# Split products in the wide attention layer: fp32 score and value products replaced by three fp32r products each, the next value projection and the context loads moved

## The reference

```python
q = jnp.einsum('bsd,ed->bse', x, wq)
k_new = jnp.einsum('bsd,ed->bse', x, wk)
v_new = jnp.einsum('bsd,ed->bse', x, wv)
k = jnp.concatenate([k_cache, k_new], axis=1)      # k_cache = v_cache = context
v = jnp.concatenate([v_cache, v_new], axis=1)
scores = jnp.einsum('bqd,bkd->bqk', q, k) * scale
attn = jax.nn.softmax(scores, axis=-1)
out = jnp.einsum('bqk,bkd->bqd', attn, v)
return jnp.einsum('bqd,ed->bqe', out, wo)
```

## Time and profile before

| | |
|---|---|
| median of 3 runs | 3709.82 us (3708.83 to 3711.08) |
| span of the profiled execution (its own time) | 3708.5 us |
| TensorE busy | 3396.1 us (92%) |
| VectorE busy | 2402.3 us (65%) |
| ScalarE busy | 1673.8 us (45%) |
| mean granted clock of TensorE | 0.963 |
| this layer | about 2993 to 3345 us |

### The profile page before, as it was taken

The page is one execution under the profiler, slowest core; times in us unless marked ns, Lnnn a source line. Parts: engine busy times, 40 slices in busy tenths (PEclk is TensorE's granted clock), DMA queues, the critical chain, the costliest instruction groups (busy, mean ns, idle before and its releaser), DMA issues. The chain is left out here.

```text
span 3708.5 us, 54381 instructions
## 1 busy us (share of the span) xinstructions
PE 3396.1 (92%) x17963; PEld 2692.7 (73%) x17976; DVE 2402.3 (65%) x6378; ACT 1673.8 (45%) x4027; POOL 955.0 (26%) x997
## 2 busy tenths in 40 slices
PE   6884999998799999999999988999999889988999
PEld 4552787786678787778787766888878656656887
DVE  4888889887576666766666657899755522228433
ACT  4553545444334434444434333788557633331222
POOL 3654444443222222332222223000323400000000
PEclk9886999999999999999999998999999899999999
DMA  5113001001100000110000006999800133333000
GB/s 219 21 19 78 0 0 46 23 0 56 51 20 20 27 20 27 65 42 21 27 20 27 19 17 218 356 406 401 290 27 2 46 118 105 117 97 102 11 10 20
DMA packets 113696, 296.11 MB, mean 80 GB/s; under 512 B 38033, under 2 KB 42129, under 8 KB 107777
## 3 DMA queue, kind: packets, MB, share of 16 engines
q1 hardware_dynamic: 107376, 276.39, 21.2%
q0 software_dynamic: 6160, 17.67, 1.6%
HBM read 251.65 MB, written 41.68 MB: 79 GB/s over the span
## 5 line engine op out<-in xcount | busy, mean ns | idle before, releaser
L40 PE MATMUL bank<-w,cross_ctx_part 128*125 128x512 f32 x1536 | 517.1, 418 | 8.1 <-DVE cross_qn L1090 4.7
L40 PEld LDWEIGHTS bank<-w,cross_ctx_part 128*125 128x125 f32 x1536 | 281.7, 187 | 93.7 <-DVE cross_kn L1090 14.7
L1000 ACT ACTIVATE cross_prob<-bank,cross_neg_max 112x375 f32<-112x375 f32 x256 | 147.2, 575 | 359.3 <-DVE cross_neg_max L1096 359.3
L40 PE MATMUL bank<-w_low,cross_ctx_part 128*125 128x512 f32 x768 | 303.7, 395 | 0.0
L40 PE MATMUL bank<-moe_wt,moe_zT 128*128 128x448 f32 x1176 | 264.0, 373 | 2.1 <-DVE moe_zT L1726 1.5
L1096 DVE TENSOR_REDUCE cross_neg_max<-bank 112x1 f32<-112x375 f32 x256 | 134.0, 524 | 198.0 <-PE bank L872 195.4
L1716 DVE TENSOR_TENSOR moe_wt<-moe_raw,moe_wt 128x1792 fp32r<-128x1792 f32 (+1 forms) x111 | 231.8, 2107 | 16.9 <-ACT moe_wt L1614 16.3
L40 PE MATMUL bank<-w,self_xq 128*112 128x512 f32 x512 | 213.7, 417 | 25.0 <-DVE w_low L595 25.0
L40 PEld LDWEIGHTS bank<-moe_wt,moe_zT 128*128 128x128 f32 x1176 | 215.1, 190 | 17.6 <-issue 1.7
L40 PE MATMUL bank<-mlp_zT,mlp_signs 128*128 128x448 f32 x1024 | 220.8, 368 | 4.7 <-DVE mlp_zT L2329 4.7
L772 POOL TENSOR_TENSOR cross_ve<-cross_mv,eps 125x4 f32<-125x4 f32 (+1 forms) x160 | 32.2, 201 | 730.4 <-DVE cross_mv L1081 730.4
(11 more groups left out here) (398 smaller groups left out, 8403.9 us busy)
## 6 DMA issues: line engine op xcount, KB each, us to landing
moe_raw<-in_moe_w SPq DMA_DIRECT2D x74, 896.0 KB, 7.3
moe_raw<-in_moe_w SPq DMA_DIRECT2D x37, 1024.0 KB, 8.2
stream<-in_L1f SPq DMA_DIRECT2D x32, 768.0 KB, 4.3
cross_ctx_raw<-in_ctxT SPq DMA_DIRECT2D x32, 750.0 KB, 4.1
wide_ctxT<-in_ctxT SPq DMA_DIRECT2D x16, 750.0 KB, 12.8
wide_ctx_rows<-in_ctx SPq DMA_DIRECT2D x16, 750.0 KB
expert_rows<-a_zeros SPq DMA_DIRECT2D x1, 8960.0 KB, 27.0
moe_zrow<-expert_rows SPq DMA_DIRECT2D x35, 256.0 KB, 7.7
```

The lines of the kernel that those rows point to most:

```text
L40: mm = pe.matmul(out, a, b, start=first and n == 0, stop=last and n == len(pairs) - 1)
L1000: op = act.activation(prob[:, t % SLOTS, i, :], score_bank(t)[0:S, i * NK:(i + 1) * NK], ACT.Exp, bias=neg_max[:, h:h + 1], accum_out=tota ...
```

## The change

Scores and value product become split products. For that, `ctxT`, the context rows, the turned q and k, v and the probabilities each get a high part (ScalarE) and a low part (VectorE). The turned keys go into one tile `allT` with the context's, padded by a zero column to 488, so that the scores are one set of 12 products. TensorE makes the v rows of b + 1 ahead of the value product of b. SyncE issues `load` (ctxT and the rows, now waiting for the low parts of the element before) ahead of `load_mlp`. The copy of the context for b + 1 stands on ScalarE between the exponential of b and the copies of q and k of b + 1; `rows_high(b + 1)` stands between `take_v(b + 1)` and the sums of b.

```diff
@@ SyncE
             def load(b):
-                wait(sp, s["scores_in_psum"], b)
+                wait(sp, s["ctxT_low"], b)
                 sp.dma_start(ctxT[:], ...).then_inc(s["ctxT_landed"], 16)
+                wait(sp, s["rows_low"], b)
+                sp.dma_start(ctx_rows[:], ...).then_inc(s["ctx_landed"], 16)
+
+            def load_mlp(b):
                 wait(sp, s["mlp_summed"], 3 * b)
                 sp.dma_start(stream[:, 0:MLP_COLS], io["L1f"][b]).then_inc(s["mlp_landed"], 16)
-                wait(sp, s["out_in_psum"], b)
-                sp.dma_start(ctx_rows[:], ...).then_inc(s["ctx_landed"], 16)
+            load(0)
             sp.wait_ge(s["w_low"], 4)
-            load(0)
+            load_mlp(0)
...
             for b in range(1, B):
                 load(b)
+                load_mlp(b)
@@ TensorE
+            def scores(b):
+                pe.wait_ge(s["ctxT_low"], b + 1)
+                pe.wait_ge(s["q_low"], b + 1)
+                pe.wait_ge(s["k_low"], b + 1)
...
+                wait(pe, s["exp_done"], b)
+                for c in range(DC):
+                    mm = product(pe, ps[3][0:S, 0:NK + 1], [h[:, c, :] for h in qT], [h[:, c, :] for h in allT],
+                                 c == 0, c == DC - 1)
+                mm.then_inc(s["scores_in_psum"], 1)
+
+            def weigh_rows(b):
+                pe.wait_ge(s["rows_low"], b + 1)
+                pe.wait_ge(s["v_low"], b + 1)
+                pe.wait_ge(s["probsT_low"], b + 1)
+                wait(pe, s["out_ready"], b)
+                for j in range(J + 1):
+                    n = JN if j < J else S
+                    mm = product(pe, ps[5][0:S, :], [h[0:n, j, :] for h in probT],
+                                 [h[:, j, :] for h in rows_part] if j < J else [h[:] for h in v], j == 0, j == J)
+                mm.then_inc(s["out_in_psum"], 1)
...
-                    wait(pe, s["probsT_ready"], 2 * b)
+                    wait(pe, s["probsT_low"], b)
...
                 pe.wait_ge(s["exp_done"], b + 1)
                 if one_more:
-                    pe.wait_ge(s["q_ready"], b + 2)
+                    pe.wait_ge(s["q_low"], b + 2)
...
-                for j in range(J + 1):
-                    n = JN if j < J else S
-                    mm = pe.matmul(ps[5][0:S, :], probT[0:n, j, :], ctx_rows[:, j, :] if j < J else v[:],
-                                   start=j == 0, stop=j == J)
-                mm.then_inc(s["out_in_psum"], 1)
                 if one_more:
+                    pe.wait_ge(s["v_low"], b + 1)
                     rows(b + 1, 2, wv, "v_in_psum")
+                weigh_rows(b)
@@ ScalarE
             def take_v(b):
                 act.wait_ge(s["v_in_psum"], b + 1)
-                act.activation(v[:], ps[2][0:S, :], ACT.Copy).then_inc(s["v_ready"], 1)
+                wait(act, s["out_in_psum"], b)
+                act.activation(v[0][:], ps[2][0:S, :], ACT.Copy).then_inc(s["v_ready"], 1)
+
+            def ctxT_high(b):
+                act.wait_ge(s["ctxT_landed"], 16 * b + 16)
+                wait(act, s["scores_in_psum"], b)
+                act.activation(allT[0][:, :, 0:KEYS], ctxT[:], ACT.Copy).then_inc(s["ctxT_high"], 1)
+
+            def rows_high(b):
+                act.wait_ge(s["ctx_landed"], 16 * b + 16)
+                wait(act, s["out_in_psum"], b)
+                act.activation(rows_part[0][:], ctx_rows[:], ACT.Copy).then_inc(s["rows_high"], 1)
...
                 if one_more:
+                    ctxT_high(b + 1)
                     take_rows(b + 1)
                     take_turned(b + 1)
...
+                if two_more:
+                    act.wait_ge(s["v_in_psum"], b + 2)
+                    z_high(b + 2)
                 if one_more:
                     take_v(b + 1)
-                if two_more:
-                    z_high(b + 2)
+                    rows_high(b + 1)
                 sum_magnitudes(b)
@@ VectorE, in step
                 dve.reciprocal(inverse[:], total[:]).then_inc(s["inverse_ready"], 1)
+                if one_more:
+                    ctxT_low(b + 1)
+                    turned_low(b + 1)
                 if not first:
                     add_out(b - 1)
+                probsT_low(b)
+                if not first:
                     measure_next(b - 1)
+                if two_more:
+                    z_low(b + 2)
...
                 dve.tensor_scalar(o[:], ps[5][0:S, :], inverse[:], None, ALU.mult).then_inc(s["out_ready"], 1)
-                if two_more:
-                    z_low(b + 2)
+                if one_more:
+                    v_low(b + 1)
+                    rows_low(b + 1)
```

More of the change, by code:

```diff
@@ L1908, in wide_attention_layer @@
              "out_ready", "outT_in_psum", "out_high", "out_low", "y_in_psum", "x_done", "mlp_landed", "mlp_summed",
-             "next_stat", "next_centre", "next_vareps", "next_rooted", "ahead_landed")
+             "next_stat", "next_centre", "next_vareps", "next_rooted", "ahead_landed", "ctxT_high", "ctxT_low", "q_low",
+             "k_low", "rows_high", "rows_low", "v_low", "probsT_low", "padded")
     s = {n: k.sem(f"wide_{n}") for n in names}
@@ L1919, in wide_attention_layer @@
         ctx_rows = sb("ctx_rows", [JN, J, D])
+        allT = [sb(f"allT{i}", [P, DC, NK + 1], F32R) for i in range(2)]
+        rows_part = [sb(f"rows_part{i}", [JN, J, D], F32R) for i in range(2)]
         q = sb("q", [S, D])
         key = sb("key", [S, D])
-        qT = sb("qT", [P, DC, S])
-        kT = sb("kT", [P, DC, S])
-        v = sb("v", [S, D])
+        qT = [sb(f"qT{i}", [P, DC, S], F32R) for i in range(2)]
+        v = [sb(f"v{i}", [S, D], F32R) for i in range(2)]
         prob = sb("prob", [S, NK])
-        probT = sb("probT", [JN, J + 1, S])
+        probT = [sb(f"probT{i}", [JN, J + 1, S], F32R) for i in range(2)]
         neg_max = sb("neg_max", [S, 1])
@@ L1947, in load @@
             def load(b):
-                wait(sp, s["scores_in_psum"], b)
+                wait(sp, s["ctxT_low"], b)
                 sp.dma_start(ctxT[:], io["ctxT"][b].rearrange("p (c n) -> p c n", c=DC)).then_inc(s["ctxT_landed"], 16)
+                wait(sp, s["rows_low"], b)
+                sp.dma_start(ctx_rows[:], io["ctx"][b].rearrange("(j p) d -> p j d", p=JN)).then_inc(s["ctx_landed"], 16)
+            def load_mlp(b):
                 wait(sp, s["mlp_summed"], 3 * b)
                 sp.dma_start(stream[:, 0:MLP_COLS], io["L1f"][b]).then_inc(s["mlp_landed"], 16)
-                wait(sp, s["out_in_psum"], b)
-                sp.dma_start(ctx_rows[:], io["ctx"][b].rearrange("(j p) d -> p j d", p=JN)).then_inc(s["ctx_landed"], 16)
+            load(0)
             sp.wait_ge(s["w_low"], 4)
-            load(0)
+            load_mlp(0)
             for m in range(MLP_SLOTS):
@@ L1964, in _ @@
         def _(pool):
+            for part in allT:
+                pool.memset(part[:, :, NK:NK + 1].bitcast(F32), 0.0).then_inc(s["padded"], 1)
             for b in range(B):
@@ L2007, in project_out @@
                 mm.then_inc(s["y_in_psum"], 1)
+            def scores(b):
+                pe.wait_ge(s["ctxT_low"], b + 1)
+                pe.wait_ge(s["q_low"], b + 1)
+                pe.wait_ge(s["k_low"], b + 1)
+                if b == 0:
+                    pe.wait_ge(s["padded"], 2)
+                wait(pe, s["exp_done"], b)
[13 more added lines that the diff above has]
+                mm.then_inc(s["out_in_psum"], 1)
             def step(b, one_more, two_more):
                 first = isinstance(b, int) and b == 0
[L2011 to L2019, removed]
+                scores(b)
                 if one_more:
@@ L2085, in take_turned @@
                 act.wait_ge(s["qT_in_psum"], b + 1)
-                act.activation(qT[:], tiled(4), ACT.Copy).then_inc(s["q_ready"], 1)
+                wait(act, s["scores_in_psum"], b)
+                act.activation(qT[0][:], tiled(4), ACT.Copy).then_inc(s["q_ready"], 1)
                 act.wait_ge(s["kT_in_psum"], b + 1)
-                act.activation(kT[:], tiled(0), ACT.Copy).then_inc(s["k_ready"], 1)
+                act.activation(allT[0][:, :, KEYS:NK], tiled(0), ACT.Copy).then_inc(s["k_ready"], 1)
             def take_v(b):
                 act.wait_ge(s["v_in_psum"], b + 1)
-                act.activation(v[:], ps[2][0:S, :], ACT.Copy).then_inc(s["v_ready"], 1)
+                wait(act, s["out_in_psum"], b)
+                act.activation(v[0][:], ps[2][0:S, :], ACT.Copy).then_inc(s["v_ready"], 1)
+            def ctxT_high(b):
+                act.wait_ge(s["ctxT_landed"], 16 * b + 16)
+                wait(act, s["scores_in_psum"], b)
+                act.activation(allT[0][:, :, 0:KEYS], ctxT[:], ACT.Copy).then_inc(s["ctxT_high"], 1)
[3 more added lines that the diff above has]
+                act.activation(rows_part[0][:], ctx_rows[:], ACT.Copy).then_inc(s["rows_high"], 1)
             def out_high(b):
@@ L2115, in step @@
```

(39 more changed lines are left out.)

## The result

The changed kernel takes 3748.7 us (median of 4 runs, 3748.1 to 3756.8) against 3710.5 us of the kernel before (4 runs): ratio 1.0098, 95% interval 1.0086 to 1.0111, which is 32 to 41 us slower. The forecast was 3746 us with a range of 3713 to 3768. The execution that was profiled is the slowest of the four (3756.8 us), and 12.4 us of its 46.6 us more than the profiled one of before stand ahead of this layer (first scores at 3005.78 in place of 2993.38 us), where the change does nothing; the layer is therefore compared by its own length.

A forecast was written before the change was run, and what follows sets the result against it. TensorE's own order bounded the kernel before; after the change, a loop through ctxT's late landing would. 19.2 + 14 x 24.9 + 20.4 = 388.2 us against 351.7, +36.5, gives 3746 us (8 in 10: 3713 to 3768).

The forecast's parts named there:

- The work without waits: TensorE's own work in one element with no new waits: 19.2 us, 2.4 us less than before.
- the 0.85 us ahead of the value product: TensorE's wait for the context rows' DMA; claimed to go because the rows load one element ahead.
- The landing of ctxT: Next element's ctxT lands 10.66 us after the scores' start, 6.3 us after the MLP tile's issue.
- The closed loop: Elements 1 to 14: the transfer burst waits for the value product's end, which depends on the burst; element 22.9 us.
- The pause: TensorE idle 4.0 us ahead of the turn of q in each element, ready at 8.7, started at 12.7.
- The clock: Low TensorE clock behind each pause: 2.0 us an element (1.4 to 2.6), making the element 24.9 us.
- The ends: Element 0 at 19.2 us in place of 21.85, element 15 at 20.4 us in place of 27.1.
- The clock did not hold: Rival: TensorE's clock stays up behind the pauses, element 22.9 us, kernel 3718 us; chance 0.12.
- The two transfers did not run abreast: Rival: ctxT lands 4.5 us after its own issue, pause 2.6 us, element 21.5, kernel 3699 us; chance 0.08.
- the share of 0.89: DMA engines' busy share ascribed to the MLP tile alone, held against the abreast rival: little left for a second transfer.
- The wait was not hidden: Rival: the wait for ctxT is hidden after all, element 19.2 us, kernel 3667 us; chance 0.06.
- ctxT did not land as late as before: Rival: ctxT lands 12.8 us after its issue as before, 6.9 us more an element, kernel 3843 us; chance 0.06.

The follow-up runs named there:

- e1: Changed kernel with SyncE issuing the context tiles of element b + 1 ahead of the MLP tile of b: 3680.4 us, ratio 0.9917 to the kernel before.
- e2: Changed kernel with copy and subtraction of the next ctxT moved behind the copies of q, k and turned q, k: 3667.1 us, 0.9893 to the kernel before.
- e7: Changed kernel with both the late copy of ctxT and the context tiles issued ahead of the MLP tile: 3686.3 us, 0.9892 to the kernel before.
- e8: Changed kernel with the late copy of ctxT, run again on a second chip: 3684.0 us, ratio 0.9895 to the kernel before.
- e6: Late-copy kernel with scores and value product as plain fp32 products over the high parts alone: 3703.3 us, ratio 0.9936 to the kernel before.
- e5: Kernel before with only the context rows' load issued ahead of the MLP tile, products left plain: 3715.4 us, ratio 0.9977 to the kernel before.
- e4: Changed kernel with SyncE loading only the first half of each MLP tile: 3724.7 us, ratio 1.0043 to the kernel before.
- e3: Changed kernel with 16 extra useless products ahead of the turn of q in elements 1 to 14: 3726.2 us, ratio 1.0041 to the kernel before.

## Why the prediction was right

**The work without waits.** Scores 2.7 us forecast, 2.65 measured (3101.42 to 3104.07); value product 2.85 forecast, 2.79 measured; v rows 2.85 and 2.86; element without new waits 19.2 forecast, 19.03 measured in e1, e2, e7 and e8. For the split products the sum had 0.6 us at the scores and 0.6 at the value product and the v rows behind it, 1.2 together; e6 shows 1.27.

**One cover was misread.** The prediction let the 0.85 us ahead of the value product go because the rows load sooner. e5 shows that the load takes away only what lies above 0.51 us; the 0.51 are ScalarE's copy of the probabilities, and what hides that is the v rows, which now stand between. The sum came out right because the change does both.

**The landing of ctxT.** Forecast 10.66 us after the scores' start, with 6.3 us between the MLP issue and the landing. Measured: ScalarE starts its copy at 10.75, and the issue is at 4.38 (forecast 4.36). The closed loop is shown by e1 and e2, which open it at two different places, and by e4, which shortens it in one place and gets the amount back.

**The pause.** 4.0 us forecast, 4.00 mean measured; e3 gives an element of 22.73 us for the pause without the clock, forecast 22.9. That is 3.70 above the 19.03: behind the pause the turn of k no longer waits for ScalarE as it does without it (0.48 us from the turn of q to the turn of k in e3, 0.85 in the earlier trace rows), which gives 0.37 of the 4.0 back. The prediction had this term.

**The clock.** 2.0 us forecast, 1.70 measured by e3 and by the busy time; over 14 elements that term was 4 us too large.

**The ends.** Here the sizes were off. Element 0 was put at 19.2 us and took 22.76: it has no output projection and no transposed output, so that without waits it is 17.03 us (e2), and its own wait for ctxT behind the five MLP tiles, with the low clock behind it, costs 5.7 us; the prediction had named that wait and given it no price beyond "18 to 22 is possible". Element 15 took 21.14 in place of 20.4:

```profile
3376.18 4.57 PE L40 MATMUL bank<-wide_wo,wide_oT 128*112 128x512 f32 x12 [2.39 <-DVE wide_oT L2189]
...
3382.78 2.31 PE L40 MATMUL bank<-wide_rows_part,wide_probT 125*112 125x512 f32 x9 [1.62 <-DVE wide_probT L2215]
```

The wait for the rows' DMA ahead of the value product is gone, as forecast, but 1.62 us stay there for the new low part of the probabilities, and the output projection waits 2.39 us, where it waited 1.39 before. The clock falls here too (mean 0.92). The prediction had the 1.62 us and the 1.0 added to the other at nothing.

**The sum.** 22.76 + 342.06 + 21.14 = 386.0 us against 388.2 forecast: +3.6 from element 0, -6.5 from the elements (the clock, and an element without waits of 19.03 in place of 19.2), +0.7 from the last. The misses cancel in part. The timed medians differ by 38.3 us, 4.0 more than the layer; that rest lies outside the layer and is in no term of the sum. So the mechanism and its sizes were right to some 2 us of the layer, and that the kernel's time came out within 3 us of the forecast is in part luck.

**The rivals.** The clock did not hold: it fell behind 14 of 14 pauses. The two transfers did not run abreast: 6.3 us from the MLP issue to ctxT's landing, where abreast would have been 4.9. The argument held against this rival was weaker than it looked: the share of 0.89 in the earlier trace rows is not of the MLP tile alone, since SyncE issued it at 3321.36 and the rows at 3321.73, both before that stretch. The wait was not hidden, and ctxT did not land as late as before.

## What to carry to other kernels

When a copy of prefetched data is put into an in-order engine's list, ask when the data land relative to what stands behind the copy, not relative to when the data are needed. A copy whose data landed more than 10 us after the scores' start cost TensorE nothing in one place of ScalarE's order and 5.4 us an element in another (24.43 against 19.03), because there the copies behind it fed TensorE. When several single-buffered transfers are issued by one queue, look for the one whose release comes last: all that stand behind it in program order inherit its date. And a pause of TensorE is to be priced with the clock behind it: here the pause made an element 3.7 us longer by itself and 5.4 with the clock.

## What the runs showed of the hardware that was not expected

Pauses of nearly the same length can cost different amounts: behind 2.65 us without work the clock stayed at 1.00, behind 2.70 us, one element later, it fell to 0.50 (e4). Length alone does not decide it there: one pause of 3.05 us left the clock at 1.00 and one of 2.62 us did not. Behind the 14 pauses of 3.69 us and more of the changed kernel it fell each time. Between such lengths a forecast has to be a share of the pauses (in e4 8 of 14), not a price for each.

The same instructions ahead of this layer do not take the same time in each run: on the first chip the profiled runs of e1 and e2 start their first scores at 3006.6 and 2994.3 us. That is a difference of 12 us before the edit can act. It is there in steps: 5.5 us at 1004 us, 11.2 us at 2650 us. The same holds on the other chip, where e7 and e8 start them at 3015.4 and 3005.1 us. Such shifts can move the medians of single kernels by some microseconds against the length of the layer (e5: 16.8 us by the profile, 5 to 12 us by the timed runs; e1 and e2: 4.3 us by the layer, 13.3 by the medians). Where they come from was not tried.
